# Gated attention and mixture-of-experts block on one core: TensorE products regrouped by type, each normalised row written once for both experts

## The reference, cut to what matters

```python
x = x + tanh(g_xattn) * xattn(layernorm(x), ctx, ctx)      # x: 32 sequences of 128 rows of 128
x = x + tanh(g_ffn)   * ffn(layernorm(x))

# xattn: rotary embedding on q and k, 16 heads of width 8
Q, K, V = heads(rope(q) @ Wq.T + bq), heads(rope(k) @ Wk.T + bk), heads(v @ Wv.T + bv)
out = softmax(Q K^T / sqrt(8)) V ;  return out @ Wo.T + bo

# ffn: 8 experts, the best 2 of each row
xn = rms_norm(x, norm_scale) ; scores = xn @ w_router.T
ids = top_k(scores, 2) ; c = softmax(scores)[ids]
val, gate = split(xn @ w_up[e].T)         # 352 each
y[e] = (val * silu(gate)) @ w_down[e].T
return sum(y[ids] * c) + x
```

## Time and profile before

| what | value |
|---|---|
| median of three runs | 574.02 us (564.71 to 576.14) |
| the profiled execution, whole | 566.83 us |
| its span, first to last instruction | 565.0 us, granted TensorE clock 0.813 on average |
| attention loop, from the first L1136 of b = 0 | 44.8 us to about 338 us |
| rest of the router, tile table, last scatters | about 338 us to 368 us |
| expert tiles | 368 us to 541 us, 2.29 us each |
| results fetched, added, stored | 541 us to 565 us |
| busy: TensorE / VectorE / ScalarE / GpSimd | 463.1 / 308.2 / 257.0 / 204.7 us |

### The profile page before, as it was taken

One profiled execution on the slowest core, in us unless ns is written; L12 is line 12 of the kernel. 1 busy time (PEld: TensorE's weight loads), 2 busy tenths in 40 slices (PEclk: granted clock), 3 DMA queues, 4 the chain that ended last, 5 costly groups with the idle time before them and its releaser, 6 DMA issues.

```text
span 565.0 us, 13155 instructions
## 1 busy us (share of the span) xinstructions
PE 463.1 (82%) x3820; PEld 302.2 (53%) x3821; DVE 308.2 (55%) x1119; ACT 257.0 (45%) x578; POOL 204.7 (36%) x196
## 2 busy tenths in 40 slices
PE   6579999989799799897979672099999999999910
PEld 2335554645455455445445342067877777778710
DVE  5275786966466467546547134145555555555525
ACT  2316575754354355444334422045555555555400
POOL 4251232334334335325411506524444444444410
PEclk9779999988578679588567555589999999999955
DMA  5524141443644203104100101221211111121049
GB/s 154 130 53 106 40 121 32 125 115 88 173 109 127 72 11 104 40 12 114 50 21 2 40 1 39 87 67 58 60 55 55 54 57 53 55 57 45 23 156 291
DMA packets 53314, 43.15 MB, mean 76 GB/s; under 512 B 7776, under 2 KB 50019, under 8 KB 53267
## 3 DMA queue, kind: packets, MB, share of 16 engines
q1 hardware_dynamic: 46834, 32.40, 21.2%
q0 software_dynamic: 4416, 8.63, 4.7%
q10 hardware_dynamic: 2016, 1.52, 1.1%
HBM read 18.45 MB, written 11.75 MB: 53 GB/s over the span
## 4 chain that ended last, share of the span: by engine, by line
PE 72%; DVE 6%; issue 5%; DMA 5%; another core or an unknown queue 4%; ACT 3%; POOL 2%; SPq 1%; ACTq 1%; POOLq 0%; DVEq 0%
PE bank L1347 9%; PE bank L1325 8%; PE bank L1327 8%; PE bank L1149 7%; PE bank L1136 6%; PE bank L1123 5%; PE bank L1337 4%; PE bank L1166 4%; DMA yl<-result_dram 2%; PE bank L1182 2%; PE bank L1183 2%; PE bank L1093 2%; PE bank L1103 2%; PE bank L1111 2%
## 5 line engine op out<-in xcount | busy, mean ns | idle before, releaser
L734 DVE TENSOR_REDUCE nmx<-bank 128x4 f32<-128x512 f32 x128 | 86.6, 684 | 79.3 <-PE bank L1123 64.9
L468 POOL DMA_INDIRECT result_dram<-ys,yi x72 | 70.4, 978 | 108.1 <-ACT ys L665 103.9
L524 ACT ACTIVATE pt<-bank 128x512 f32<-128x512 f32 x128 | 72.7, 596 | 32.5 <-PE bank L1136 32.4
L411 POOL DMA_INDIRECT slots_dram<-xr,slu x64 | 62.5, 976 | 32.5 <-issue 17.2
L1347 PEld LDWEIGHTS bank<-wf_sb,hT 128*128 128x128 f32 (+1 forms) x432 | 57.3, 192 | 21.3 <-issue 17.2
L1021 DVE TENSOR_TENSOR hh<-sg,bank 128x352 f32<-128x352 f32 x72 | 37.5, 521 | 55.9 <-PE bank L1327 45.1
L1347 PE MATMUL bank<-wf_sb,hT 128*128 (+1 forms) x432 | 61.5, 279 | 2.0 <-DVE hT L1031 1.8
L1149 PE MATMUL bank<-pt,v 128*9 128x128 f32 x1024 | 60.8, 316 | 0.3
L1123 PE MATMUL bank<-ks,qs 62*128 62x128 bf16 x512 | 57.5, 243 | 3.9 <-DVE nmx L734 2.1
L1325 PE MATMUL bank<-wf_sb,xT 128*128 x144 | 55.7, 469 | 0.0
L1327 PE MATMUL bank<-wf_sb,xT 128*128 x144 | 55.0, 464 | 0.0
(11 more groups left out here) (154 smaller groups left out, 757.4 us busy)
## 6 DMA issues: line engine op xcount, KB each, us to landing
qs<-parts SPq DMA_DIRECT2D x48, 128.0 KB
ks<-parts SPq DMA_DIRECT2D x42, 128.0 KB
xs<-slots_dram SPq DMA_DIRECT2D x72, 66.0 KB
yl<-result_dram SPq DMA_DIRECT2D x8, 512.0 KB, 6.0
wf_sb<-in_wup SPq DMA_DIRECT2D x8, 352.0 KB
x_sb<-in_x SPq DMA_DIRECT2D x8, 256.0 KB, 4.1
ctx_sb<-in_ctx_in SPq DMA_DIRECT2D x8, 256.0 KB, 3.8
out<-x_sb SPq DMA_DIRECT2D x8, 256.0 KB, 4.6
```

Of the source, the lines that this page charges most:

```text
L411: nc.gpsimd.indirect_dma_start(out=slots_dram, out_offset=bass.IndirectOffsetOnAxis(ap=slu[:, c % 2, k, kk:kk + 1], axis=0), in_=xr[:, c % ...
L468: nc.gpsimd.indirect_dma_start(out=result_dram, out_offset=bass.IndirectOffsetOnAxis(ap=yi[:, r:r + 1], axis=0), in_=ys[:, r, :], in_offse ...
L524: nc.scalar.activation(pt[:, 4 * g:4 * g + 4, :], STB[g % 2][:, :].rearrange("p (h s) -> p h s", h=4), ACT.Exp, scale=SCORE_SCALE).then_in ...
L734: nc.vector.tensor_reduce(nmx[:, b % 2, at:at + 4], SB[g % 2][:, :].rearrange("p (h s) -> p h s", h=4), AX.X, ALU.max, negate=True).then_i ...
```

## The change

1. **TensorE's order in the loop.** The bf16 products stand together: groups 0 and 1 of `scores_by_key`(b), then groups 0 and 1 of `scores`(b+2); later groups 2 and 3 of both. The float32 `weighted_values` stand apart from them; 2 and 3 are at the end of the step. The projection stands before `weighted_values`(b, 0).
2. **The bias of the output projection** becomes three bf16 rows (`bop3`), multiplied by three bf16 rows of ones, after the main product. Eight chained VectorE instructions (`bias_parts`) make these before the loop; one did before.
3. **One row for both experts.** `xr` is [128, 2, 4, 136]: the values, twice the row number (float32), both gates, both expert numbers. The 8 indirect DMAs per chunk read the same row for both slots. `rows` and `last_rows` write half as much.
4. **Per tile**, `result_rows` compares the two expert numbers with the tile's (`mine`), adds the second comparison to the row number and chooses the gate: four instructions, two of which wait for the ones before, where there were two independent ones. The tile table is broadcast to 128 partitions (`ebt`).
5. **The routing moves back.** `transpose_rows` goes from u = 2 to u = 3, `router` and `take_scores` from u = 3 to u = 0 of the next chunk, `choose_*` to u = 1 and 2, `positions` to u = 2, `place*` and `probabilities` to u = 2 and 3. The loops are three to four empty steps longer. `scatter` sends k = 0, 1, 2 (six DMAs) at u = 0 and k = 3 at u = 1. `statistics` moves from u = 2 to u = 0; `remainder` and `high` of the key projection come earlier in their step.

```diff
 # TensorE, order of step b
                 if real(b + 2):
                     scores(b + 2, 0)
+                    scores(b + 2, 1)
                 if real(b + 1):
                     transpose_maximum(b + 1)
                 if real(b - 1):
                     heads_by_query(b - 1)
-                if real(b + 2):
-                    scores(b + 2, 1)
-                if real(b):
-                    weighted_values(b, 0)
-                    scores_by_key(b, 2)
...
                 if real(b):
-                    weighted_values(b, 1)
+                    weighted_values(b, 0)
+                    scores_by_key(b, 2)
                     scores_by_key(b, 3)
                 if real(b + 2):
                     scores(b + 2, 2)
+                    scores(b + 2, 3)
+                if real(b):
+                    weighted_values(b, 1)
                 if real(b - 1):
                     transpose_attended(b - 1)
-                if real(b + 2):
-                    scores(b + 2, 3)
+                if u == 1 and there(c + 2):
+                    transposes_ctx(c + 2, PR)
+                if u == 3 and there(c - 1):
+                    transpose_rows(c - 1)
+                if u == 0 and there(c - 2):
+                    router(c - 2, b)
+                if u == 2 and there(c - 2):
+                    positions(c - 2, b)
                 if real(b):
                     weighted_values(b, 2)
+                    weighted_values(b, 3)
                 if real(b - 1):
                     project_out(b - 1)
...
 # project_out
-                mm(SMALL[:, D:2 * D], ones[0:1, :], bop[:, :], start=True, stop=False)
-                mm(SMALL[:, D:2 * D], onT[:, :], wo_sb[:, :], start=False, stop=True).then_inc(pe_o, 1)
+                mm(SMALL[:, D:2 * D], onT[:, :], wo_sb[:, :], start=True, stop=False)
+                mm(SMALL[:, D:2 * D], onesb[0:3, :], bop3[:, :], start=False, stop=True).then_inc(pe_o, 1)
...
 # GpSimd, order of the scatters
                     if there(c - 3):
-                        scatter(c - 3, (2, 3))
+                        scatter(c - 3, (0, 1, 2))
+                if u == 1:
+                    if there(c - 1):
+                        power2(c - 1)
+                    if there(c - 3):
+                        scatter(c - 3, (3,))
-            scatter(NCH - 3, (2, 3))
+            scatter(NCH - 3, (0, 1, 2))
             power2(NCH - 1)
+            scatter(NCH - 3, (3,))
             scatter(NCH - 2, range(CH))
             scatter(NCH - 1, range(CH))
...
 # VectorE, result_rows
-                nc.vector.tensor_copy(yi[:, r:r + 1], xs[:, r, D:D + 1].bitcast(U32))
-                nc.vector.tensor_copy(yc[:, r:r + 1], xs[:, r, D + 1:D + 2]).then_inc(fd_i, 1)
+                nc.vector.tensor_scalar(mine[:, r, :], xs[:, r, D + 3:D + 5], ebt[:, bass.ds(t, 1)], None, ALU.is_equal)\
+                    .then_inc(fd_m, 1)
+                dve.wait_ge(fd_m, 2 * t + 1)
+                nc.vector.tensor_tensor(yi[:, r:r + 1], xs[:, r, D:D + 1], mine[:, r, 1:2], ALU.add)
+                nc.vector.tensor_scalar(yc0[:, r:r + 1], xs[:, r, D + 1:D + 2], mine[:, r, 0:1], None, ALU.mult).then_inc(fd_m, 1)
+                dve.wait_ge(fd_m, 2 * t + 2)
+                nc.vector.scalar_tensor_tensor(yc[:, r:r + 1], xs[:, r, D + 2:D + 3], mine[:, r, 1:2], yc0[:, r:r + 1],
+                                               ALU.mult, ALU.add).then_inc(fd_i, 1)
```

More of the change, by code:

```diff
@@ L442, in _ @@
                     if there(c - 3):
-                        scatter(c - 3, (2, 3))
[L444 to L450, removed]
+                        scatter(c - 3, (0, 1, 2))
[4 more added lines that the diff above has]
+                        scatter(c - 3, (3,))
+                if u == 2 and there(c + 2):
+                    rotate_k(c + 2)
                 if u == 3:
@@ L592, in _ @@
             middle(1, 0)
-            for b in range(B + CH + 1):
+            for b in range(B + 2 * CH):
                 c, u = b // CH, b % CH
@@ L614, in _ @@
                     high(c + 2, 0, PR)
+                if u == 3 and there(c + 2):
+                    high(c + 2, 1, PR)
+                if u == 3 and there(c - 1) and c < NCH:
+                    rows(c - 1, (2, 3))
+                if real(b):
+                    exponent(b, 2)
+                if u == 2 and there(c - 1):
+                    rows(c - 1, (0, 1))
                 if real(b - 1):
                     attended(b - 1)
-                if u == 2 and there(c - 1) and c < NCH:
-                    rows(c - 1, (2, 3))
-                if u == 0 and there(c - 2):
+                if u == 1 and there(c - 2):
                     expert_exp(c - 2)
@@ L916, in _ @@
             remainder(1, 1, PR)
-            for b in range(B + CH + 2):
+            for b in range(B + 2 * CH):
                 c, u = b // CH, b % CH
@@ L926, in _ @@
                     maximum(b + 2, 1)
-                if u == 0 and there(c - 2):
+                if u == 1 and there(c - 2):
                     choose_values(c - 2)
+                if u == 2 and there(c - 2):
+                    choose_masks(c - 2)
                 if real(b - 1):
@@ L932, in _ @@
                     shift(c + 2)
-                if u == 1 and there(c - 2):
+                if u == 2 and there(c - 2):
+                    choose_sum(c - 2)
+                if u == 3 and there(c - 2):
                     place_rows(c - 2)
@@ L979, in _ @@
                     rotate_q(c + 2)
-                if u == 3 and there(c + 2):
-                    remainder(c + 2, 1, PR)
             ch = Chain(dve, d_tc, 0)
```

136 lines of the change are left out of this document (68 added, 68 removed).

## The result

The changed kernel took 546.92 us (median of four runs, 544.06 to 547.29). The kernel before, run beside it on the same chip, took 571.88 (four runs, 564.71 to 576.14). The ratio is 0.9631, with a 95% interval of 0.954 to 0.9722: 3.7% faster. The forecast was 540 us in a range of 516 to 570.

What follows compares the result with a forecast made beforehand. TensorE was taken to bound the loop, with low clock and late completions lengthening later chunks. 566.8 - 12.7 (chunks 0 to 2) - 21.4 (chunks 3 to 7) + 2 (after the loop) + 5 (tiles) = 539.7, forecast 540 us, range 516 to 570.

Steps and rivals of the forecast that it cites:

- Grouping: TensorE's loop step: four pairs replace two pairs and four singles, 0.82 us less per step at full clock, 1.44 at low.
- Bias: TensorE's bias product in each loop step: 0.33 us less at the full clock, 0.58 at the low one.
- Chunks 0 to 2: First three chunks of the loop: 8.7 us from shorter steps plus 4.0 from later scatters, 12.7 us less.
- because the first scatters fall into its second half: Chunk 2 takes 34.2 us against chunk 1's 29.8 for this reason; scatters starting in chunk 3 save 4.0 us.
- the 0.55 us that I gave it: Loss per chunk in the loop to VectorE's strict order, add_attention waiting for a later projection; between nothing and 3 us.
- Chunks 3 to 7: Later chunks of the loop at a mean clock of 0.7: 29.9 us saved less 5 x 1.7, 21.4 us less.
- The hold-up: TensorE's completions arrive late during GpSimd's indirect DMA runs: about 5 us per chunk, left as it is.
- the clock pays it back: Rival for chunks 3 to 7: TensorE idles more often, clock stays at 0.5, slower at 588 us; chance 0.12.
- the clock rises: Rival: scatters together disturb one stretch per chunk, mean clock 0.85, some 20 us more saved, 520 us; chance 0.17.
- After the loop: GpSimd's remaining indirect DMAs set the end behind the loop: 2 us more, bounds 0 to 6.
- Chunk 7 starts 1.5 to 2 us later: Behind the loop, chunk 7's indirect DMAs start later, after two of chunk 5 and eight of chunk 6; 2 us taken.
- Tiles: Expert tiles: four VectorE instructions exceed the room by 0.14 us; 0.07 us per tile, x 72, 5 us more.

Runs made afterwards that it cites:

- kernel 1: Kernel before with only TensorE's products regrouped into pairs of one kind, scatters in their old places: 551.1 us, ratio 0.9646.
- kernel 2: Kernel before with only the bias changed, three bf16 rows behind the projection for one float32 row ahead of it: 574.5 us, ratio 1.0045.
- kernel 9: Kernel before with the regrouped products and the bf16 bias, nothing else: 544.9 us, ratio 0.9555.
- kernel 6: Whole change with the old float32 bias row put back ahead of the projection: 563.7 us, ratio 0.989.
- kernel 5: Regrouping alone plus the change's scatter places, six indirect DMAs then two, one chunk later: 553.1 us, ratio 0.9706.
- kernel 3: Whole change with hidden_down issued ahead of result_rows on VectorE in the expert tiles: 541.9 us, ratio 0.9474.
- kernel 4: Whole change with all 64 scatter indirect DMAs issued behind the loop, eight row buffers: 570.2 us, one run.
- kernel 10: Regrouping and bf16 bias on the kernel before, each chunk's run of four indirect DMAs issued as two pairs in two steps: 539.4 us, ratio 0.942.

## Why the prediction was right, and where its terms were off

**The sum, 540 against 547.** The loop came out as forecast (34.1 us less predicted, 32.3 measured), and so did the tiles; the 7.5 us or so between the sum and the profiled execution are 4.8 us more behind the loop, 1.8 less gained in the loop, 0.7 ahead of it and 0.2 in the tiles. That the loop came out so well is partly luck: chunks 0 to 2 gained 6.2 us less than forecast and chunks 3 to 7 gained 4.3 more, so two errors nearly cancel.

**Grouping: right.** Pairs of eight 0.24 us apart replaced singles of 0.32. Alone it was worth 20 us where the terms give 19. Nothing was added for the changes of tiling mode that also vanish, and kernel 1's loop is 18.7 us shorter where the terms without them give 19; no run prices them apart.

**Bias: right in the sum, wrong as a term.** I priced it per step and added it to the grouping. The product itself lost 0.26 us at the full clock and not 0.33, and 0.50 at the low one and not 0.58. But its worth depends on the order around it: 0 us in the old step (2), some 5 or 6 on top of the regrouping (9 against 1), 15 to 17 in the whole change (6). The step's length is not TensorE's sum of work: in chunk 1 its busy time fell by 4.7 us and the chunk by 1.8. That a chain through ScalarE and VectorE gives back the rest is my reading of the waits; no run tests it. Why the last order makes so much more of the bias than kernel 9's is not settled either. No run changed the routing's place and kept the rest.

**Chunks 0 to 2: 12.7 forecast, 6.5 measured.** The failed step is "because the first scatters fall into its second half": I read chunk 2's 34.2 us as the price of two pairs of indirect DMAs. Kernel 1 kept them there and took 30.7, kernel 5 removed them and took 30.5. What chunk 2 had before was a stretch at the low clock (mean 0.85, now 0.94). The other steps gained 1.8 us in chunk 1 and 0.3 in chunk 0. Chunk 1 took 28.0 us, above the 25 to 27 that I had named. VectorE, at 81%, may take more than the 0.55 us that I gave it, but no run shows that. Chunk 0 had a stretch at the low clock (mean 0.93); in kernel 3, with the same loop, it took 24.8 us at 0.99.

**Chunks 3 to 7: 21.4 forecast, 25.7 measured.** The hold-up was left at 5 us per chunk; kernel 4 puts it at 6.5 in the new kernel, and no run has its price in the old one. I had also named waits of 3 to 7 us once per chunk; there are 21 waits on "remote". I had priced runs of 2, 2 and 4 that become 6 and 2, but in chunks 6 and 7 the old kernel issues eight in one run (276.00 to 285.89 and 311.94 to 321.84): those two chunks give 13.8 of the 25.7 us, where kernel 1, which keeps the runs of eight, gives 4.5 there, and kernel 9 gives 6.1. Kernel 5, without runs of eight in the loop but with the old routing, gives 4.0, so it is not their absence alone, and what brings the rest stays open. What I had not taken in is the clock: 0.66 to 0.79 in chunks 3 to 6 before, 0.77 to 0.83 now. The rival "the clock pays it back" was wrong by sign: TensorE's idle share of chunk 3 rose from 11% to 24%, and the granted clock rose with it, to 0.81. The Trainium skill, TensorE: Matmul & The Clock Gate, section HAM oscillation, says that waits between groups of matmuls throttle the clock again. It speaks of single waits, and I had carried it over to the share of idle time, which these rows do not bear out; without the indirect DMAs and the waits beside them (kernel 4) the clock was 0.94, in line with the page. The milder rival "the clock rises" was half true: it expected a mean of 0.85 where it is 0.77 over chunks 3 to 7, from 0.70.

**After the loop: 2 forecast, 6.8 measured, above the bound of 6.** Two steps failed. "Chunk 7 starts 1.5 to 2 us later": the last indirect DMA is 3.8 us later relative to the last statistics. The new places leave more of chunk 5 (3.5 us more behind the loop in kernel 5), and the third buffer takes back 1.7 in the trace, so the two-buffer wait, which I had not priced, is a part. And I had said nothing of the padding rows that SyncE and ScalarE write. They are issued when the slot counts are known, which now falls into the middle of sixteen indirect DMAs without a break. ScalarE's four, before and after:

```profile
354.06 3.56 ACTq L637 DMA_DIRECT2D slots_dram<-pad_sb  x4
```

```profile
324.28 11.83 ACTq L639 DMA_DIRECT2D slots_dram<-pad_sb  x4
```

SyncE's four went from 6.02 to 13.90 us, and the first tile's load waits for them. With 64 indirect DMAs in one run (kernel 4) they took 17.32 and 25.22.

**Tiles: 5 forecast, 5.2 measured.** 0.077 us per tile, where 0.07 was worked out. Kernel 3 removes it.

**Half of the row writes: nothing,** right. ScalarE's busy time in chunk 3 went from 19.89 to 19.51 us.

**Ahead of the loop,** I let the eight bias instructions fit into VectorE's wait. The first maxima start at 35.95 and not at 35.61. The 0.7 us by which the loop starts later are not shown to be theirs, since kernel 6, which has one instruction in their place, starts it at 45.37. One of the eight took 3.30 us, while GpSimd filled buffers from 31.65 to 35.19:

```profile
31.97 3.30 DVE L699 TENSOR_SCALAR bop<-bhigh,con 3x128 f32<-3x128 bf16 x1
```

## What to carry to other kernels

Two cuts in one engine's step can't be priced apart and added: the cheaper bias was worth 0, 6 or 15 us by the order around it. Time what is left with the edit undone (kernel 6) as well as with the edit alone (kernel 2) before calling it useless. Where small GpSimd indirect DMAs run beside a busy loop, look up in the trace in what runs they are really issued, and break the long ones: the same eight per chunk cost 6.5 us as six and two, and 4 as four pairs, each in its place of the step. Halving runs of four gained nothing that the trace shows (kernel 10); breaking a run of eight into four, two and two came with 8 us less in its chunk, and making six and two of the old places (kernel 5) gained nothing. And instructions added to an in-order engine belong behind the work that others wait for: one swap was worth 5 us.

## What was not expected of the hardware

While GpSimd issues indirect DMAs, TensorE's completions reach the engines that wait for them late, by 3.5 us in the rows above. It is not the traffic, since twice the bytes per row change nothing, and it is less beside short runs (waits of up to 10.0 us beside eight, of up to 5.3 to 7.0 beside six). SyncE's own register and issue steps, 0.02 to 0.06 us each in the chain before, take 0.70 each in the changed kernel beside the run of sixteen. They turn slow at 325.57, ten us into the run, and quick again at 338.25, 2.6 us after its last instruction has ended (335.60):

```profile
325.53 0.04 issue
325.57 0.64 SPq L332
326.21 0.71 issue
```

The Trainium skill, DMA: Bandwidth & Descriptors, section SWDGE vs HWDGE vs iDMA, says that DMAs issued from SyncE and ScalarE are immune to the interference that GpSimd's descriptor writing meets at its rings. These rows show another kind, on the issuing side, with a factor of 2.3 to 3.3 on the padding rows. Through which resource GpSimd delays the others no run here shows.
